# Expert weights in long rows through an address list, and the order of choice and slots, in a three-layer kernel

## The reference, cut to what matters

```
x = x + xattn(layernorm(x), ctx)          # cross attention, 32 x 32 queries, 257 keys, 16 heads
x = x + attn(layernorm(x))                # self attention, 32 tokens a sequence
x = x + ffn(layernorm(x))
def ffn(z):                               # D = 512, P = 9 experts, DM = 128
    m = mix[0]*z[:-1] + mix[1]*z + mix[2]*z[1:]
    h = einsum('bsd,pdm->bspm', m, W1) + b1
    paths = einsum('bspm,pmd->bspd', h, W2) + b2
    scores = tanh(m @ Wo1 + bo1) @ Wo2 + bo2
    idx = argmax(scores)                  # one expert for each token
    return layernorm(z + paths[idx]) * gamma + beta
```

## Time and profile before

| | |
|---|---|
| median of 3 runs | 771.59 us (771.25 to 773.29) |
| profiled execution | 770.54 us, its span 768.8 us |
| TensorE busy | 722.8 us, 94% of the span |
| VectorE, ScalarE, GpSimd busy | 373.9, 335.6, 203.2 us |
| HBM read and written | 46.93 and 10.49 MB |

### The profile page before, as it was taken

One profiled execution on the slowest core, in us unless ns is written; L12 is line 12 of the kernel. 1 busy time (PEld: TensorE's weight loads), 2 busy tenths in 40 slices (PEclk: granted clock), 3 DMA queues, 4 the chain that ended last, 5 costly groups with the idle time before them and its releaser, 6 DMA issues. The chain is left out here.

```text
span 768.8 us, 20525 instructions
## 1 busy us (share of the span) xinstructions
PE 722.8 (94%) x8158; PEld 561.6 (73%) x8158; DVE 373.9 (49%) x978; ACT 335.6 (44%) x727; POOL 203.2 (26%) x297
## 2 busy tenths in 40 slices
PE   4999999999999999999999999989999997989894
PEld 3777788778778777877877877767877775756552
DVE  5545424424433443443444255665677773632564
ACT  3445435444453543444445355443444443423442
POOL 0001001000010010010010020287667855331865
PEclk9999999999999999999999999999999998767998
DMA  9211110110111011011012103410000063254760
GB/s 331 77 55 56 56 57 2 56 55 8 47 55 55 0 55 55 0 55 55 9 46 55 55 0 109 126 17 16 15 28 29 30 206 108 74 202 182 235 221 25
DMA packets 21877, 55.97 MB, mean 73 GB/s; under 512 B 6194, under 2 KB 11058, under 8 KB 18886
## 3 DMA queue, kind: packets, MB, share of 16 engines
q1 hardware_dynamic: 18246, 40.64, 15.7%
q0 software_dynamic: 3584, 14.69, 5.4%
HBM read 46.93 MB, written 10.49 MB: 75 GB/s over the span
## 5 line engine op out<-in xcount | busy, mean ns | idle before, releaser
L96 PE MATMUL pj<-W_both 128*128 128x512 f32 x544 | 221.7, 407 | 10.1 <-DVE W_both L595 10.1
L98 PE MATMUL pj<-W_both 128*128 128x512 f32 x544 | 213.4, 392 | 0.0
L97 PE MATMUL pj<-W_both 128*128 128x512 f32 x544 | 212.6, 391 | 0.0
L96 PEld LDWEIGHTS pj<-W_both 128*128 128x128 f32 x544 | 102.6, 189 | 43.3 <-issue 23.6
L236 POOL COPY q_b<-Q_T 128x128 f32 (+1 forms) x32 | 9.3, 292 | 415.4 <-PE tp L359 348.9
L98 PEld LDWEIGHTS pj<-W_both 128*128 128x128 f32 x544 | 102.5, 188 | 22.7
L97 PEld LDWEIGHTS pj<-W_both 128*128 128x128 f32 x544 | 102.9, 189 | 19.0
L493 ACT ACTIVATE K<-pj,bk 128x512 f32<-128x512 f32 x64 | 44.2, 691 | 135.6 <-PE pj L98 135.6
L654 DVE CUSTOM_DVE_ANT_0 m_flat<-sc,mask 128x257 f32<-128x257 f32 x64 | 24.7, 424 | 116.1 <-PE tp L359 94.9
L508 ACT ACTIVATE p_flat<-m_flat,nmax 128x257 f32<-128x257 f32 x128 | 63.8, 501 | 25.5 <-DVE nmax L654 25.4
L500 ACT ACTIVATE V<-pj 128x512 f32<-128x512 f32 x64 | 38.2, 597 | 73.2 <-PE pj L98 71.9
(11 more groups left out here) (342 smaller groups left out, 1174.2 us busy)
## 6 DMA issues: line engine op xcount, KB each, us to landing
raw<-ctx_dram SPq DMA_DIRECT2D x15, 1024.0 KB, 4.8
raw<-w_dram SPq DMA_DIRECT2D x4, 1024.0 KB, 4.8
experts<-w_dram SPq DMA_DIRECT2D x9, 256.0 KB, 4.3
experts<-w_dram SPq DMA_DIRECT2D x3, 768.0 KB, 6.7
x_nat<-x_dram SPq DMA_DIRECT2D x2, 1024.0 KB, 12.2
rows<-z3s SPq DMA_DIRECT2D x8, 256.0 KB, 2.5
rows<-x_nat SPq DMA_DIRECT2D x8, 256.0 KB, 2.7
rows<-xm SPq DMA_DIRECT2D x8, 256.0 KB, 2.1
```

Of the source, the lines that this page charges most:

```text
L96: eng.matmul(out, a_hi, b_hi, start=first, stop=False)
L97: eng.matmul(out, a_lo, b_hi, start=False, stop=False)
L98: return eng.matmul(out, a_hi, b_lo, start=False, stop=last)
```

## The change: what it does, and the diff

W1 is loaded by one DMA for three experts, 6 KB a partition, in the order in which it lies in DRAM (for each quarter of D, three experts side by side). Its offsets differ then from those of W2: `weight_at` has two columns, DVE's `weight_offsets` makes the second (e/3 part times 1536 plus e%3 times 128), `slot_lists` makes one more list, `at` is twice as long, and TensorE loads a second register for each slot, ahead of `outputs`. bo2 is added by DVE in `choose`, no longer by a matmul. The result has four buffers instead of three. `gate_scores(1)`, the row transposes, census and evacuations stand in another order; `idle` has five matmuls; slot 0's hidden layer comes before slot 1's transposes; slot 14 is finished before slot 15 is centred. The code of variance and root on GpSimd is the same in both kernels.

```diff
@@ sync
             def load(i):
                 n = 3 * D
-                for j in range(3):
-                    eng.dma_start(w1_all[:, i * n + j * D:i * n + (j + 1) * D].rearrange("p (c m) -> p c m", c=CT),
-                                  io["w1"][i].rearrange("p (c e m) -> p c e m", c=CT, e=3)[:, :, j, :]).then_inc(exw_in, 16)
+                eng.dma_start(w1_all[:, i * n:(i + 1) * n], io["w1"][i]).then_inc(exw_in, 16)
@@ results
-            return xm[:, 1, k % 3 * D:(k % 3 + 1) * D]
+            return xm[:, 1, k % NH * D:(k % NH + 1) * D]
@@ tensor
             def gate_scores(g):
-                if g == 0:
-                    eng.wait_ge(tables, TABLES)
                 for i in range(b - a):
-                    eng.matmul(to, th_of(g)[:, i * P:(i + 1) * P], wo2[:, :], start=True, stop=False)
-                    mm = eng.matmul(to, ones[0:1, :], bo2[0:1, :], start=False, stop=True)
+                    mm = eng.matmul(to, th_of(g)[:, i * P:(i + 1) * P], wo2[:, :], start=True, stop=True)
@@ slot_lists
-                eng.matmul(found[0:1, NS:2 * NS], weight_at[0:NB, :], listed[:, :], start=True, stop=True)
+                for i in range(2):
+                    eng.matmul(found[0:1, (1 + i) * NS:(2 + i) * NS], weight_at[0:NB, i:i + 1], listed[:, :], start=True, stop=True)
@@ hidden, outputs
-                w_at = eng.value_load(at[0:1, k:k + 1], min_val=0, max_val=(E - 1) * D)
+                w_at = eng.value_load(at[0:1, NS + k:NS + k + 1], min_val=0, max_val=2 * 3 * D + 2 * P)
...
-                    mm = eng.matmul(h_bank(k), x_T(k)[:, c * P:(c + 1) * P], w1_all[:, bass.ds(w_at + c * P, P)],
+                    mm = eng.matmul(h_bank(k), x_T(k)[:, c * P:(c + 1) * P], w1_all[:, bass.ds(w_at + c * 3 * P, P)],
...
-            def outputs(k, w_at):
+            def outputs(k):
+                w_at = eng.value_load(at[0:1, k:k + 1], min_val=0, max_val=(E - 1) * D)
@@ order on tensor
             weighted_sum(NT + 1)
-            gate_scores(1)
             positions(0)
             out_proj(NT + 2)
+            gate_scores(1)
             rows_transposes(0)
             gate(2)
             rows_transposes(1)
             map_tiles(0)
             positions(1)
+            rows_transposes(2)
+            rows_transposes(3)
             z3_transposes(NT + 2)
             gate_scores(2)
-            rows_transposes(2)
+            rows_transposes(4)
+            rows_transposes(5)
             gate(3)
-            rows_transposes(3)
-            rows_transposes(4)
+            rows_transposes(6)
             gate_scores(3)
-            rows_transposes(5)
             map_tiles(1)
             positions(2)
+            rows_transposes(7)
             census()
-            rows_transposes(6)
             ranks()
-            rows_transposes(7)
             map_tiles(2)
             slot_lists()
-            idle(4)
+            idle(5)
             x_transposes(0)
-            x_transposes(1)
-            w_at = hidden(0)
+            hidden(0)
             for k in range(1, NS):
+                if k == 1:
+                    x_transposes(1)
                 h_transpose(k - 1)
-                if k + 1 < NS:
+                if k + 1 < NS and k > 1:
                     x_transposes(k + 1)
-                next_at = hidden(k)
-                outputs(k - 1, w_at)
+                hidden(k)
+                if k == 1:
+                    x_transposes(2)
+                outputs(k - 1)
@@ order on scalar
-            mix_parts(NT + 1, (1, 0))
+            mix_parts(NT + 1, (1,))
             o2_split(NT + 1)
-            mix_parts(NT + 1, (2,))
+            mix_parts(NT + 1, (0, 2))
             rows_evac(0)
             tanh(2)
             z3_make(NT + 2)
-            rows_evac(1)
+            for u in range(1, 4):
+                rows_evac(u)
             mix_end()
...
             xT_evac(0)
+            h_evac(0)
             xT_evac(1)
-            h_evac(0)
@@ vector
             def weight_offsets():
...
+                ch3.link(eng.tensor_scalar(at_1, at_2, 1.0 / CT, None, ALU.mult))
+                for third in range(1, 3):
+                    ch3.link(eng.tensor_scalar(row_of, at_2, float(third * 3 * D), float(3 * D - 3 * P), ALU.is_ge, ALU.mult))
+                    ch3.link(eng.tensor_tensor(at_1, at_1, row_of, ALU.add))
             def choose(g):
+                ch3.link(eng.tensor_tensor(got, lists[g][:, 0:n * E].rearrange("p (t e) -> p t e", t=n),
+                                           bo2[:, :].unsqueeze(1).broadcast_to([P, n, E]), ALU.add))
             def centre(k):
-                need(eng, stored[k % 3], k // 3 * 16)
+                need(eng, stored[k % NH], k // NH * 16)
@@ order on vector
-            for k in range(NS):
+            for k in range(NS - 1):
                 residual(k)
                 centre(k)
                 if k:
                     finish(k - 1)
+            residual(NS - 1)
+            finish(NS - 2)
+            centre(NS - 1)
             finish(NS - 1)
```

More of the change, by code:

```diff
@@ L937, in self_attention_and_experts @@
         slot_in = [sem(f"slot_in{i}") for i in range(RING)]
-        stored = [sem(f"stored{i}") for i in range(3)]
+        stored = [sem(f"stored{i}") for i in range(NH)]
         TABLES = 18
@@ L1216, in _ @@
             scatter(NS - 1)
-            for i in range(3):
-                eng.wait_ge(stored[i], len(range(i, NS, 3)) * 16)
+            for i in range(NH):
+                eng.wait_ge(stored[i], len(range(i, NS, NH)) * 16)
         @block.tensor
@@ L1408, in positions @@
                 a, b = PLACED[q]
+                if q == 0:
+                    eng.wait_ge(tables, TABLES)
                 to = places[q][:, 0:(b - a) * E]
@@ L1450, in slot_lists @@
                 eng.matmul(found[:, 0:NS], tokens_T[:, :], listed[:, :], start=True, stop=True)
-                eng.matmul(found[0:1, NS:2 * NS], weight_at[0:NB, :], listed[:, :], start=True, stop=True)
-                eng.matmul(found[0:KB, 2 * NS:3 * NS], expert_of[0:NB, :], listed[:, :], start=True, stop=True).then_inc(found_pe, 1)
+                for i in range(2):
+                    eng.matmul(found[0:1, (1 + i) * NS:(2 + i) * NS], weight_at[0:NB, i:i + 1], listed[:, :], start=True, stop=True)
+                eng.matmul(found[0:KB, 3 * NS:4 * NS], expert_of[0:NB, :], listed[:, :], start=True, stop=True).then_inc(found_pe, 1)
             def idle(n):
-                eng.wait_ge(exw_in, 13 * 16)
+                eng.wait_ge(exw_in, 7 * 16)
                 for _ in range(n):
@@ L1719, in _ @@
             z3_make(NT + 2)
-            rows_evac(1)
+            for u in range(1, 4):
+                rows_evac(u)
             mix_end()
-            rows_evac(2)
+            rows_evac(4)
+            rows_evac(5)
             tanh(3)
-            for u in range(3, NT):
-                rows_evac(u)
+            rows_evac(6)
+            rows_evac(7)
             map_evac()
             xT_evac(0)
+            h_evac(0)
             xT_evac(1)
-            h_evac(0)
             for k in range(1, NS):
                 hT_evac(k - 1)
-                if k + 1 < NS:
+                if k + 1 < NS and k > 1:
                     xT_evac(k + 1)
                 h_evac(k)
+                if k == 1:
+                    xT_evac(2)
                 if k > 1:
@@ L1928, in choose @@
                 n = b - a
-                got = lists[g][:, 0:n * E].rearrange("p (t e) -> p t e", t=n)
+                got = gs[:, 0:n, :]
                 eng.wait_ge(gs_done, g + 1)
                 need(eng, counted, a)
+                ch3.link(eng.tensor_tensor(got, lists[g][:, 0:n * E].rearrange("p (t e) -> p t e", t=n),
+                                           bo2[:, :].unsqueeze(1).broadcast_to([P, n, E]), ALU.add))
                 ch3.link(eng.tensor_reduce(top[:, 0:n], got, AX.X, ALU.max))
```

27 lines of the change are left out of this document (13 added, 14 removed).

## The result

The changed kernel takes 763.90 us in the median of 4 runs (763.79 to 764.82); the kernel before, run beside it, 771.42 (771.01 to 773.29). The ratio is 0.990, 95% interval 0.9883 to 0.9918: 7.5 us faster. I had expected 766.8, in 761.5 to 771.6, and faster with 0.76. So direction and range held, but the expected value was 2.9 us too high, and the largest part of the gain arises by the path of my first rival. The profiled execution took 763.95 us, its span is 762.2.

The account below looks back on a forecast made before the run. Behind 626 us, TensorE was taken to pace the gate stage and a ring from gather to scatter the slot loop. Terms summed to -4.8 us: 770.5 to 765.7, median 1.05 above, so 766.8, range 761.5 to 771.6.

Parts of the forecast that it names:

- first rival: Slots 0 and 1: the granted clock does not fall at 693.4, some 4 us more gained, 762.8 us; chance 0.27.
- Weights in long rows: Gate matmuls: longer load rows remove TensorE's hole in the middle; -0.7 us, bounds 0 and -2.6.
- Gate scores without bias: Gate scores: dropping the 8 bias passes of 16 starts the weighted sum earlier; -1.4 us.
- o_hi earlier: Gate stage, ScalarE: o_hi starts at the weighted sum's end, so the last projection comes sooner; -1.3 us, bounds 0 and -1.8.
- Row transposes and lists: From last projection to slot 0's transposes: reordered transposes and lists; -0.3 us, bounds -3.0 and +1.5.
- offsetting pair: Before slot 0: last rows store leaving earlier, -0.7 us, against a fifth idle matmul, +0.7; together 0.
- Slots 0 and 1: First slots: hidden(0) no longer stands behind slot 1's transposes and begins earlier; -1.3 us, bounds 0 and -5.5.
- Second register load: Each slot, ahead of outputs: one more TensorE register load, hidden by running matmuls; +0.1 us, bounds 0 and 4.0.
- Second rival: Slots: the second register load isn't hidden, +4.0 us in place of +0.1, 770.7 us; chance 0.15.
- Offset table: Five small DVE operations ahead of the next step's statistics delay the head norm; +0.5 us, bounds 0 and 0.7.
- The end: Last slots: finishing slot 14 before centring slot 15 clears DVE during GpSimd's last root; -0.4 us, bounds 0 and -0.8.
- Third rival: Loop of slots: the clock falls there, +2.2 us for each such slot, 775.6 us with four; chance 0.09.

Follow-up runs that it names:

- e_short: Changed kernel with W1 loaded in nine DMAs of 512 B runs into the new places instead of long rows; 764.76 us.
- e_late: Changed kernel with the last two loads of expert weights issued behind `z_rows(6)`, some 20 us later; 761.64 us.
- e_order: Changed kernel with slots 0 to 2 in the old order on TensorE and ScalarE, five idle matmuls kept; 767.48 us.
- e_both: Changed kernel with four idle matmuls and the old order of slots 0 and 1; 769.12 us.
- e_table: Changed kernel with the offset table made later, behind the last x2 statistics on DVE; 762.84 us.
- f_nofill: Changed kernel with the last two weight loads behind `z_rows(6)` and the offset table behind the last x2 statistics; 757.88 us.
- e_idle4: Changed kernel with four idle matmuls again instead of five; 764.17 us.
- e_three: Changed kernel with three result buffers again instead of four; 765.40 us.
- f_alone: Kernel before with nothing but the new order of slots 0 to 2 and the fifth idle matmul; 767.11 us.
- f_fill: f_nofill with three matmuls without use, of 256 columns, added in the gaps of slots 0 and 1; 761.31 us.

## Why the prediction was right or wrong

*Weights in long rows*, -0.7: 0 (2.60 and 2.64 us of hole; e_short 764.76 us). The step that failed is "the loads lengthen the first hole by at most 2.60-1.59=1.0 us", and with it the view that fewer microseconds of loading make it shorter: the loads are all of it (e_late), and their speed does not shorten it (3.19 us in e_short, 2.08 to 3.14 in the eight with long rows, 2.51 and 2.60 in the other two with short ones). The rule of the Trainium skill ("DMA: Bandwidth & Descriptors", Specifications) that 512 B reach line rate gave the right time, 0, but not for its reason: from 632 to 635.5 the kernels with 512 B runs moved 280 to 341 GB/s and those with 6 KB runs 381 to 416.

*Gate scores without bias*, -1.4: right by the row that it was read from, since without the bias and with the gate matmuls at half clock, as before, the weighted sum starts 1.5 us earlier behind the scores, and e_T is "just in time" (waits of 0.20 and 0.24 us in e_order and e_both, none in e_late, e_table and f_nofill). In the kernel after the gate matmuls ran at full clock, which alone is -1.2, and the bias added only -0.3 before TensorE met the same floor and waited 1.21 us. Together that is -1.5: the two savings do not add.

*o_hi earlier*, -1.3: from the weighted sum to the projection 4.26 before, 2.74 after, -1.5. Right, o_hi starts at the end of the sum (657.09 and 657.05).

*Row transposes and lists*, -0.3: from the last projection to the first gather 25.06 and 25.03 us, 0; then from the gather to slot 0's transposes 5.27 and 5.98, +0.7, as the fifth idle matmul at half clock reaches beyond the rows' arrival. Of my offsetting pair only this half came. That the last rows store "was probably the last to arrive" was wrong: the gather starts 0.94 us behind the end of to_slot in both kernels (682.43+0.17 and 683.54 after), as in all 14 profiles, although the stores now leave some 3 us earlier.

*Slots 0 and 1*, -1.3: -5.1. The step that failed is the mechanism of the term: it let hidden(0) start earlier and left the clock at half. Hidden(0)'s part was -1.9 (3.19 and 1.29 us behind the transposes), and the other 3.2 us, by subtraction, are the clock (e_idle4 prices it at 3.6). This was the first rival, priced at -4 more than the forecast and given 0.27; its mechanism came in 8 of the 10 profiled executions of the new order (e_table left out) and in none of the 3 of the old. My argument against it, "there is still little TensorE work", looked at the amount of work. What goes with the clock in all 13 profiles is the wait of slot 1's transposes for their gather: 0 to 0.49 us in the 8 that kept it (0 in the kernel after), 0.95 to 3.16 in the 5 that didn't (1.67 before). That is a match over 13 executions; no run sets this wait by itself. The rows showed that wait, and that hidden(0) would fill it; this should have had half the chance or more.

*Second register load*, +0.1: 0; outputs start right behind what stands ahead of them (695.86, 699.22, 702.59). Second rival refuted. *Four buffers*, 0: right, 5.1 us of waits gone, and nothing of it resolved in the loop (e_three). *"Variance and root"*: same code, no change, right.

*Offset table*, +0.5: 0.57 in its step, as worked out (waits of 0.73 less a cover of 0.2), and 0.8 more a step later that no row of before could show.

*The end*, -0.4: the last root took 0.56 instead of 0.96, and from its start to the last scatter it is 2.27 us instead of 2.99: -0.7, within the bounds. f_alone, which has the old order at the end, supports the step: its last root took 0.56 too, but the operation ahead of it, while DVE finished slot 14 (759.38 to 760.13), took 0.51 where it takes 0.18 after.

```profile
759.68 0.51 POOL L1195 TENSOR_SCALAR root_in<-squares 128x1 f32<-128x1 f32 x1
```

From the start of this operation to the last scatter it is 3.26 us before, 3.17 in f_alone and 2.54 after. From root 1 to the last root another 0.8 us went, which I had not forecast; which slot waits for its gather differs between executions (51.47 and 50.65 us for this stretch before and after, 51.0 to 52.0 in the other six executions whose clock did not fall there).

*Third rival*, clock falls in the loop: not in the changed kernel, but in five other profiled executions (e_idle4, e_order, e_both, e_late, f_alone), 53.7 to 55.6 us from the gather of slot 7 to the last scatter against 50.6 to 52.2 in the others. I gave it 0.09 as something that the change would cause; it stands in e_order with the old order and in f_alone with the new, and not in the kernel after, which has f_alone's order too. So it goes with the execution at least as much as with the code.

Two things stood in no term. Ahead of any changed instruction the kernel after is 0.9 us late (the projections of the step with the table begin at 584.35 and 585.24); that is drift between executions, since the scores of this step begin anywhere from 590.2 to 592.8 us in the 14 profiles. And the second half of the gate matmuls ran at full clock, 1.99 us instead of 3.28; from their start to the gate scores that is -1.2. The sum as measured: 0.9 drift, 1.4 table, 0.2 in the steps behind it, 0 long rows (-0.1), -1.2 gate matmuls, -0.3 gate scores, -1.5 o_hi, +0.7 idle matmul, -5.1 slots 0 and 1, -0.8 loop, -0.7 end: -6.5 of rounded terms, for 6.66 at the last scatter. My -4.8 came near partly by luck: long rows gave nothing (-0.7 forecast), the table's place cost 0.9 to 1.1 more than I had put, the idle matmul 0.7 without the gain that was to offset it, and the clock in slots 0 and 1 outweighed all of this.

Of the three signs that I had set for being wrong, two came. The first gather starts only 0.74 us earlier, not 2 or more (and the last projection 0.71, where I had said about 3): the long rows gave nothing, the table cost more, and the drift came on top. The loop from gather 7 to the last scatter changed by 1.54 us (52.17 and 50.63), just over the 1.5. The third, a gap of the outputs behind hidden, did not come.

## What to carry to other kernels

Where a profile shows the granted clock fall behind a wait, the first thing to ask of a reorder is not how many microseconds of waiting it removes but whether it splits the long wait ahead of a dense stretch: putting hidden(0) into the middle of the wait for slot 1 was worth some 5 us in the profiles and 3 to 6 in the times, of which only 1.9 were waiting. A saved matmul is to be followed to the next input of its engine: two savings ahead of the same input, here the bias and the full clock of the gate matmuls, do not add beyond the point at which that input is ready. A comparison of two kernels for one term needs the clock to be the same in both profiles just ahead of it. And a hole that ends with "issue" beside bulk loads is tested by moving the loads: this took the hole of 2.6 us out, while making the loads faster took nothing.

## What the runs showed of the hardware that I had not expected

- TensorE stood still without a releaser for 2.08 to 3.19 us in the midst of four equal matmuls in each of the 11 kernels whose weights were loading then (280 to 416 GB/s from 632 to 635.5), and not at all in the three (e_late, f_fill, f_nofill) in which the DMA engines were idle. That the engine's instructions come late through the same DMA engines would fit: the DMA view counts a packet of a queue of the kind "instruction" (0.02 MB) in the first half us of the hole, from 635.5 in the kernel before and from 638.0 in the kernel after, and one from 635.0 in e_late, without a hole. No run shows whose instructions it brings.
- The granted clock falls at other times in other executions of the same kernel. TensorE was at 1.2 GHz from 640.2 to 643.6, 657.3 to 664.1 and 677.8 to 688.0 in one execution of the changed kernel, and from 639.4 to 646.3, 653.1 to 663.3 and 677.0 to 687.2 in the next. The executions of one kernel lie 4 to 12 us apart, and within each of the twelve runs those with the higher mean clock were the faster ones (correlations of -0.83 to -0.97).
- The first gather on GpSimd starts 0.94 us after the end of the DVE operation that makes its list, in all 14 profiles, whether the issue of the last rows store ended 1.5 us ahead of that end (before, 681.88 and 683.34) or 3.9 us (after, 678.75 and 682.60).
